# Part of the routing moved into sweep 3, two input pieces loaded later, and a shorter first piece in the last stage

## The chip, the cores and the metric

The kernel runs on one NeuronCore of a Trainium2 chip. The metric is the device time of one execution in microseconds (us), median of several runs. The engines are TensorE (PE, with its weight loads PEld), VectorE (DVE), ScalarE (ACT) and GpSimd (POOL); SyncE (SP) here only issues DMA transfers.

## What is computed

A graph layer, a top-2 mixture of eight experts, a second graph layer, and a small integer operation on the result. `_layernorm` is over the 256 columns of a row.

```python
x = x + gnn0(_layernorm(x), adj, W0, b0)          # A @ (x @ W + b) / deg[:, None]
x = x + ffn(_layernorm(x)[None], Wg, bg, W1, b1, W2, b2)[0]
x = x + gnn1(_layernorm(x), adj, WL, bL)          # relu(adj_norm @ x @ W.T + b)
x = x + shift_op(_layernorm(x)[None])[0]
# in ffn:
gate_scores = jax.nn.softmax(xt @ Wg + bg, axis=-1)
topk_scores, topk_idx = jax.lax.top_k(gate_scores, 2)
topk_scores = topk_scores / jnp.sum(topk_scores, axis=-1, keepdims=True)
h = gelu(xt @ W1[e] + b1[e]);  expert_out = h @ W2[e] + b2[e]
```

x is 4096 x 256, adj is 4096 x 4096, float32.

## The kernel before

Rows of x are held as 32 tiles of 128 rows. The program has three blocks, with a barrier of all engines between two of them.

The first block makes graph layer one in four sweeps. A sweep makes the sums of 1024 output rows (8 tiles): TensorE goes over the 32 tiles of adj (512 KB each, loaded by SP into a ring of 8) and multiplies them with the normalised rows `feat0`, held as a high and a low f16 half. Sweep 0 makes `feat0` on the way: x comes in five pieces (4, 4, 8, 8, 8 tiles); of each piece VectorE makes the statistics and normalised rows, ScalarE the high half, GpSimd the low half. SP's queue is written out by hand: `X_AFTER` says behind which adj tile a piece of x is issued, and `ROOT_BEFORE` before which row ScalarE makes a piece's square root. The sums of a sweep are split in two halves (ScalarE `sum_hi`, VectorE `sum_lo`) and projected with W0 during the next sweep; the projections of sweep 2 (tiles 16 to 23) run behind tiles 20 to 27 of sweep 3. Those of sweep 3 (tiles 24 to 31) come after it, when VectorE has made `sum_lo` from `sum_hi` (L579, `low_sums(3)`). While it waits TensorE runs 16 idle matmuls (`keep_busy`).

A projection has ten more columns than its 256; eight of them carry a part of the expert logits and go to `tail`. The other part of the logits, from x itself, is in `xg`. After a group of eight tiles `row_roots` makes the factor `r1` of its layer norm; in its middle it gives `ve` to ScalarE (L749) and gets the root back. VectorE's order at the end of sweep 3 is `row_roots(2)`, `degrees` of the last group (three small instructions, L714 to L716), `low_sums(3)`, eight tiles of `add_late_mean` (L733) and `row_stats`, `row_roots(3)`, and then the routing.

The routing begins with the logits of all 32 tiles, 256 columns to a partition (8 experts by 32 tiles), and two rounds of `pick` (L804 to L819), which find the best and the second best expert. `logit`, `key` and `score` lie in PSUM banks. ScalarE copies the eight columns of `tail` into `logit` first (L1005). TensorE then makes the ranks of the tokens, VectorE the place of each token, and sixteen batches of one-hot matrices, until `tokens` is ready; GpSimd waits for it and starts the first gathers of the next block (L535, L342).

Beside it ScalarE and GpSimd go on by their own orders. From the last `ve` on ScalarE runs two W2 units (`high_middle`), rows 16 to 23 (`normalise`, `high_late_row`), two units, rows 24 to 31, and the other units. GpSimd makes the low half of each: L514, two instructions of 1024 columns for two units, and L495, one of 256 columns for a row. Both read two operands in SBUF.

The second block runs the experts over slots of 256 tokens. The third makes graph layer two in five groups (8, 8, 8, 4, 4 tiles). It reloads x in the same five `PIECES`, and has the chain of statistics, root, `scaled` (VectorE), high half (ScalarE) and low half (GpSimd, L1554) again, where GpSimd also puts in the self edges of the first eight tiles (L1540, L1542). `scaled` has two buffers: VectorE scales tile n only when GpSimd has done tile n - 2. TensorE needs the low half of tile j to begin tile j.

Of the kernel before, what the change touches and what calls it, by code (L numbers as in the profile page):

```python
# [72 lines left out]
def program(nc, x, adjT, W0, b0, Wg, bg, W1, b1t, W2, b2, WL, bL, identity, upper, out):  # L73
# [176 lines left out]
    rows_early = w("rows_early", [P, 4, 2 * D], F16)  # L250
    xn8 = w("xn8", [P, G, D], F32)
    w = Region(SUM_AT, SUMS_END)
    row_hot = [w(f"row_hot{i}", [P, HOTS, P], F16) for i in range(2)]
    blk_hot = [w(f"blk_hot{i}", [P, HOTS, BLOCKS], F16) for i in range(2)]
    chosen16 = [w(f"chosen16{k}", [P, NT, E], F16) for k in range(2)]
    mix = w("mix", [P, NT, E], F32)
    running = w("running", [P, NT + 1, E], F32)
    best = [w(f"best{k}", [P, NT], F32) for k in range(2)]
    nearest = w("nearest", [P, NT], F32)
    end_at = w("end_at", [P, E], F32)  # L260
# [7 lines left out]

    logit, key, score = (pb[i][:, 0:NT * E].rearrange("p (n e) -> p n e", e=E) for i in (3, 4, 5))
    count_ps = pb[6][:, 0:P]  # L270
# [5 lines left out]
    small = iter(range(0, 512, NT))  # L276
    gap_top = pb[7][:, (at := next(small)):at + NT]
    share = [pb[7][:, (at := next(small)):at + NT] for k in range(3)]
# [48 lines left out]
    def over_tiles(ap):  # L327
        return ap.unsqueeze(1).broadcast_to([P, NT, E])
# [19 lines left out]
    PIECES = ((0, 4), (4, 4), (8, 8), (16, 8), (24, 8))  # L348
    X_AFTER = {0: 1, 3: 2, 8: 3, 14: 4}
    ROOT_BEFORE = {0: 0, 4: 1, 7: 2, 15: 3, 22: 4}  # L350

    with nc.Block(no_gpsimd_drain=True) as block:
# [188 lines left out]
        def _(v):  # L541
# [258 lines left out]
            st = Steps(v, sem("v_route"))  # L800
            v.wait_ge(sem("numbers_taken"), 4 + 2 * E)
            v.wait_ge(sem("xg_taken"), 2)
            v.wait_ge(sem("gates_copied"), 1)
            st.link(v.tensor_tensor(logit, logit, over_experts(rdeg[:, :]), ALU.mult))  # L804
            st.link(v.tensor_tensor(logit, logit, xg[:, :, :], ALU.add))
            st.link(v.tensor_tensor(logit, logit, over_experts(r1[:, :]), ALU.mult))
            st.link(v.tensor_tensor(logit, logit, over_tiles(bg_all[:, :]), ALU.add))

            def pick(scores, best, one_hot):
                st.link(v.tensor_reduce(best, scores, AX, ALU.max))  # L810
                st.link(v.tensor_tensor(key, scores, over_experts(best), ALU.is_equal))
                st.link(v.tensor_tensor(key, key, over_tiles(rev[:, :]), ALU.mult))
                st.link(v.tensor_reduce(nearest[:, :], key, AX, ALU.max))
                st.wait()
                v.tensor_tensor(one_hot, key, over_experts(nearest[:, :]), ALU.is_equal).then_inc(sem("choice_ready"), 1)

            pick(logit, best[0][:, :], chosen16[0][:, :, :])
            v.wait_ge(sem("choice_ready"), 1)
            st.link(v.scalar_tensor_tensor(out=score, in0=chosen16[0][:, :, :], scalar=-BIG, in1=logit, op0=ALU.mult, op1=ALU.add))  # L819
            pick(score, best[1][:, :], chosen16[1][:, :, :])  # L820
            st.link(v.tensor_reduce(gap_top, score, AX, ALU.max))
            st.wait()
            v.tensor_tensor(gap[:, :], gap_top, best[0][:, :], ALU.subtract).then_inc(sem("gap_ready"), 1)
# [4 lines left out]
            v.wait_ge(sem("choice_ready"), 2)  # L828
            st.wait()
# [75 lines left out]
        def _(a):  # L905
# [123 lines left out]
        def _(pe):  # L1029
# [106 lines left out]
            pe.wait_ge(sem("choice_ready"), 1)  # L1136
            pe.wait_ge(sem("x1_ready"), NT)
# [365 lines left out]
    with nc.Block(no_gpsimd_drain=True) as block:  # L1503

        @block.sync
        def _(sp):
            def load_x2(g):
                at, tiles = PIECES[g]
                sp.dma_start(x_sb[:, at:at + tiles, :], x2_v[:, at:at + tiles, :]).then_inc(sem(f"x_loaded{g}"), 16)
# [7 lines left out]
            load_x2(0)  # L1517
            for g in range(1, len(PIECES)):
# [46 lines left out]
        def _(v):  # L1565
# [88 lines left out]
            st = Steps(v, sem("v_norm2"))  # L1654
            for g, (at, tiles) in enumerate(PIECES):
                v.wait_ge(sem(f"x_loaded{g}"), 32)
# [26 lines left out]
        def _(a):  # L1683
# [17 lines left out]

            for g, (at, tiles) in enumerate(PIECES):
# [76 lines left out]
```

## Time and profile before

| | us |
|---|---|
| median of 3 runs | 1015.05 (1014.02 to 1015.86) |
| profiled execution, its own time | 1014.64 |
| its span, first to last instruction | 1012.8 |
| PE busy | 927.3 (92%) |
| DVE busy | 604.5 (60%) |
| POOL busy | 428.3 (42%) |
| ACT busy | 400.9 (40%) |
| mean granted TensorE clock | 0.961 of full |

The profile lists busy time, waits and their releasers for one execution. A timeline row gives the start, the time from first start to last end, engine, line, operation, and in brackets the idle time before it and what ended it. Times count from the first instruction. The granted clock is 1.00 at 2.4 GHz and 0.50 at 1.2 GHz. Sweep 3 ends at 264.5 us, the last gathers of the first block are issued at 322.44 us and the last stage begins at 734 us.

### The profile page before, as it was taken

To read this page: it belongs to the slowest core of one execution; us is meant where nothing else is said; L and a number is where in the kernel's file an instruction comes from. 1 tells how busy PE (TensorE), PEld (TensorE's weight loads), DVE (VectorE), ACT (ScalarE), POOL (GpSimd) and SP (SyncE) were. 2 spreads that over 40 slices of the span, in tenths; PEclk is the share of its full clock that TensorE was granted. 3 is DMA by queue.
4 is the path that set the end of the run, shared out by engine and by line. 5 is a ranking of instruction groups with operands and counts; after the bars stand their busy time and mean duration, and the time that the engine had idled before them with its cause. 6 is when DMAs were issued, how large, how long until landed. Compare 5 with 4: busy or idle time off the path is not lost. (4 is left out here: it accounts for less than half of the span.)

```text
span 1012.8 us, 21659 instructions
## 1 busy us (share of the span) xinstructions
PE 927.3 (92%) x6593; PEld 608.3 (60%) x6594; DVE 604.5 (60%) x1938; ACT 400.9 (40%) x837; POOL 428.3 (42%) x437
## 2 busy tenths in 40 slices
PE   8999999999715999999999999999279999999994
PEld 5354445444403898998898899898234454544442
DVE  7736996897797666566556556556167151341644
ACT  5858777477795532322332332333013101010111
POOL 3464756515585254455455455455454300200110
PEclk9999999999956999999999999999789999999997
DMA  9989999899876433233233332323299979875770
GB/s 334 411 302 344 345 357 332 282 360 367 281 243 185 120 50 53 43 49 53 45 47 53 47 47 53 47 42 53 43 361 402 358 236 327 264 262 167 242 264 25
DMA packets 91578, 199.93 MB, mean 197 GB/s; under 512 B 14241, under 2 KB 47266, under 8 KB 91394
## 3 DMA queue, kind: packets, MB, share of 16 engines
q1 hardware_dynamic: 74482, 168.37, 47.0%
q0 software_dynamic: 17040, 30.87, 15.0%
q8 instruction: 29, 0.48, 0.2%
q14 instruction: 27, 0.22, 0.1%
HBM read 177.05 MB, written 22.16 MB: 197 GB/s over the span
## 5 line engine op out<-in xcount | busy, mean ns | idle before, releaser
L1041 PE MATMUL bank<-adj_f,feat 128*128 128x512 f16 x1024 | 237.8, 387 | 4.1 <-DMA adj_f<-in_adjT 2.7
L1327 ACT ACTIVATE act_f<-bank,b_sb 128x256 f32<-128x256 f32 (+1 forms) x312 | 122.5, 450 | 255.1 <-PE bank L1258 255.1
L1258 PE MATMUL bank<-rT,experts 128*128 128x256 f16 (+1 forms) x1872 | 191.2, 263 | 2.5 <-DVE rT L1366 2.5
L1270 PE MATMUL bank<-experts,act_h 128*128 (+1 forms) x1680 | 189.1, 273 | 0.0
L1728 PE MATMUL bank<-adj_g,feat 128*128 128x512 f16 x768 | 179.7, 388 | 1.2 <-POOL feat L1554 1.2
L1258 PEld LDWEIGHTS bank<-rT,experts 128*128 (+1 forms) x1872 | 168.8, 99 | 19.8 <-DVE rT L1366 2.9
L1041 PEld LDWEIGHTS bank<-adj_f,feat 128*128 128x128 f16 x1024 | 96.9, 96 | 129.9 <-DMA adj_f<-in_adjT 4.7
L1270 PEld LDWEIGHTS bank<-experts,act_h 128*128 128x128 f16 x1680 | 163.0, 98 | 18.3
L923 ACT ACTIVATE spent<-adj_f 128x1024 f16<-128x1024 f32 x128 | 135.1, 1055 | 23.3 <-DMA adj_f<-in_adjT 17.5
L1185 POOL DMA_INDIRECT x_rows<-y,token x70 | 113.4, 1621 | 63.9 <-issue 54.6
L1728 PEld LDWEIGHTS bank<-adj_g,feat 128*128 128x128 f16 x768 | 74.4, 97 | 94.5 <-issue 2.1
L1354 DVE TENSOR_TENSOR act_h<-act_f,act_h 128x512 f16<-128x512 f32 x140 | 97.1, 693 | 4.8
L646 DVE CUSTOM_DVE_ANT_0 products<-agg,wg_turned 128x256 f32<-128x256 f32 x192 | 98.3, 575 | 0.0
L342 POOL DMA_INDIRECT rows<-ln_rows,token x68 | 69.5, 1022 | 40.1 <-DVE gates L1361 22.3
L1352 DVE CAST act_h<-act_f 128x512 f16<-128x512 f32 x140 | 59.9, 428 | 24.5 <-PE bank L1270 23.9
L1591 DVE SCALAR_TENSOR_TENSOR agg_lo<-bank,agg_hi 128x512 f16<-128x512 f32 x16 | 10.0, 683 | 94.0 <-ACT agg_hi L1690 94.0
L466 POOL TENSOR_SCALAR unit_f<-unit_f 128x1024 f32<-128x1024 f32 x16 | 45.9, 2866 | 42.3 <-ACT experts L928 42.3
L1728 PE MATMUL bank<-adj_early,feat 128*128 128x512 f16 x256 | 59.6, 388 | 0.9 <-issue 0.9
L1361 DVE COPY gates<-rows (+1 forms) x32 | 5.9, 184 | 83.7 <-PE bank L1241 83.7
L192 ACT ACTIVATE std<-mv,eps_col 128x8 f32<-128x8 f32 x10 | 3.0, 301 | 131.5 <-DVE mv L1573 131.5
L1198 POOL COPY token<-tokens 128x10 int32 (+1 forms) x35 | 11.8, 338 | 86.2 <-DMA x_rows<-y,token 86.2
L1540 POOL TENSOR_TENSOR adj_g<-adj_g,grow 128x128 f32<-128x128 f32 x24 | 11.2, 465 | 83.0 <-DMA adj_g<-in_adjT 83.0
(274 smaller groups left out, 986.5 us busy)
## 6 DMA issues: line engine op xcount, KB each, us to landing
adj_f<-in_adjT SPq DMA_DIRECT2D x128, 512.0 KB, 7.1
adj_g<-in_adjT SPq DMA_DIRECT2D x72, 512.0 KB, 6.0
adj_early<-in_adjT SPq DMA_DIRECT2D x24, 512.0 KB, 6.8
adj_g<-in_adjT SPq DMA_DIRECT2D x48, 256.0 KB, 3.1
unit_f<-in_W SPq DMA_DIRECT2D x16, 512.0 KB, 6.8
stage<-in_W SPq DMA_DIRECT2D x12, 512.0 KB, 6.0
x_ring<-in_x POOLq DMA_DIRECT2D x16, 256.0 KB, 6.9
x_rows<-agg SPq DMA_DIRECT2D x4, 1024.0 KB, 8.4
```

Source lines behind the costliest of these rows:

```text
L342: pool.indirect_dma_start(rows[:, r, :], None, ln_rows[:, :], bass.IndirectOffsetOnAxis(ap=indices[:, at + r:at + r + 1], axis=0)).then_in ...
L466: pool.tensor_scalar(unit_f[u % 2][:, :], unit_f[u % 2][:, :], WS, None, ALU.mult).then_inc(sem("unit_scaled"), 1)
L646: gate_steps.did(v.tensor_tensor_reduce(out=products[:, k % PRODUCTS, :], in0=agg[:, n, :], in1=wg_turned[:, e, :], scale=1.0, scalar=0.0, ...
L923: a.activation(spent[:, :], adj_f[j % RING][:, :], ACT.Copy, accum_out=degp[:, s, j:j + 1]).then_inc(sem("deg_ready"), 1)
L1041: last = pe.matmul(mine(s)[ib * DC + c][:, :], feat0[:, j, h, c * P:(c + 1) * P], adj_0[j % RING][:, ib * HALF_SWEEP:(ib + 1) * HALF_SWEEP ...
L1185: pool.indirect_dma_start(x_rows[:, :], bass.IndirectOffsetOnAxis(ap=token[:, r:r + 1], axis=0), y[:, r, :], None, compute_op=ALU.add).the ...
L1258: last = pe.matmul(pb[2 + q][:, k * SLOT + at:k * SLOT + at + width], w1_part(mine_e * DC + (f // FQ * W2_UNIT0 + c), wh)[:, (f % FQ) * P: ...
L1270: last = pe.matmul(pb[6 + r][:, 0:D], act_h[:, ah, f, r * P:(r + 1) * P], experts[:, ds(e[r] * DC + (W2_UNIT0 + f // UH), 1), wh, (f % UH) ...
L1327: last = a.activation(act_f[q][:, k, at:at + width], pb[2 + q][:, k * SLOT + at:k * SLOT + at + width], ACT.Gelu, bias=b1_sb[:, ds(mine_e ...
L1352: v.tensor_copy(hi, act_f[q][:, :, :]).then_inc(sem("act_hi_ready"), 1)
L1354: v.tensor_tensor(act_h[:, 1, 2 * q:2 * q + 2, :], act_f[q][:, :, :], hi, ALU.subtract).then_inc(sem("act_h_ready"), 1)
L1728: last = pe.matmul(mine(s)[ib * DC + c][:, :], feat[:, j, h, c * P:(c + 1) * P], adj_1[b][:, ib * HALF_SWEEP:(ib + 1) * HALF_SWEEP], start ...
```

## The change

Three edits. First, the logits and both picks of tiles 0 to 23 are made by VectorE in sweep 3, between `row_roots(2)` and `degrees`, and those of tiles 24 to 31 after `row_roots(3)`; this is one function `choose`, which works in SBUF on `tail`, `xg`, `scores` and, for `nearest`, `dinv`. The reduction L821 and ScalarE's copy L1005 are gone; TensorE waits for the third and fourth choice. Second, in sweep 0 the x pieces 3 and 4 are issued behind adj tiles 10 and 16, where it was 8 and 14. Third, the last stage loads x in pieces of 2, 6, 8, 8 and 8 tiles.

```diff
-    X_AFTER = {0: 1, 3: 2, 8: 3, 14: 4}
+    X2_PIECES = ((0, 2), (2, 6), (8, 8), (16, 8), (24, 8))
+    X_AFTER = {0: 1, 3: 2, 10: 3, 16: 4}
...
+            def choose(first, end, turn):
+                tiles, n = slice(first, end), end - first
+                logit, held, second = xg[:, tiles, :], tail[:, tiles, 2:2 + E], scores[:, 0:n, :]
...
+                def pick(values, k):
+                    choice.link(v.tensor_reduce(best[k][:, tiles], values, AX, ALU.max))
+                    choice.link(v.tensor_tensor(held, values, by_tile(best[k]), ALU.is_equal))
+                    choice.link(v.tensor_tensor(held, held, by_expert(rev[:, :]), ALU.mult))
+                    choice.link(v.tensor_reduce(nearest[:, tiles], held, AX, ALU.max))
+                    v.tensor_tensor(chosen16[k][:, tiles, :], held, by_tile(nearest), ALU.is_equal).then_inc(sem("choice_ready"), 1)
+
+                choice.link(v.tensor_tensor(held, held, by_tile(rdeg), ALU.mult))
+                choice.link(v.tensor_tensor(logit, held, logit, ALU.add))
+                choice.link(v.tensor_tensor(logit, logit, by_tile(r1), ALU.mult))
+                choice.link(v.tensor_tensor(logit, logit, by_expert(bg_all[:, :]), ALU.add))
+                pick(logit, 0)
+                v.wait_ge(sem("choice_ready"), 2 * turn + 1)
+                choice.link(v.scalar_tensor_tensor(out=second, in0=chosen16[0][:, tiles, :], scalar=-BIG, in1=logit,
+                                                   op0=ALU.mult, op1=ALU.add))
+                pick(second, 1)
...
             row_roots(2)
...
+            choose(0, 3 * G, 0)
             degrees(3 * G, G)
             low_sums(3)
...
-            st.link(v.tensor_tensor(logit, logit, over_experts(rdeg[:, :]), ALU.mult))
...
+            choose(3 * G, NT, 1)
+            v.tensor_tensor(gap[:, :], best[1][:, :], best[0][:, :], ALU.subtract).then_inc(sem("gap_ready"), 1)
...
-            a.wait_ge(sem("tail_taken"), G)
-            a.copy(logit, tail[:, :, 2:2 + E]).then_inc(sem("gates_copied"), 1)
```

VectorE at the end of sweep 3, before. The first row is the end of `row_roots(2)` and the last is `low_sums(3)`; `gates` holds the shift of the rows here.

```order
L757 TENSOR_TENSOR r_73<-nt_81,rstd 128x8
L759 SCALAR_TENSOR_TENSOR gates<-mv,r_73 128x8
L714 TENSOR_REDUCE dg<-degp 128x8
L715 TENSOR_SCALAR dg<-dg 128x8
L716 RECIPROCAL rdeg<-dg 128x8
L579 SCALAR_TENSOR_TENSOR sum_lo<-bank,sum_hi 128x512 x4
```

The same place after the change:

```order
L767 SCALAR_TENSOR_TENSOR gates<-mv,r_73 128x8
L817 TENSOR_TENSOR tail<-tail,rdeg 128x24x8
L818 TENSOR_TENSOR xg<-tail,xg 128x192
L819 TENSOR_TENSOR xg<-xg,r_73 128x192
L820 TENSOR_TENSOR xg<-xg,bg_all 128x192
L811 TENSOR_REDUCE best_157<-xg 128x24
L812 TENSOR_TENSOR tail<-xg,best_157 128x24x8
...
L815 TENSOR_TENSOR chosen_161<-tail,dinv 128x192
L722 TENSOR_REDUCE dg<-degp 128x8
L723 TENSOR_SCALAR dg<-dg 128x8
L724 RECIPROCAL rdeg<-dg 128x8
L587 SCALAR_TENSOR_TENSOR sum_lo<-bank,sum_hi 128x512 x4
```

Fifteen instructions of 192 columns (24 tiles by 8 experts) now stand between `row_roots(2)` and `degrees`, and so ahead of `low_sums(3)`.

VectorE at the start of the routing, before (`bank` is PSUM):

```order
L804 TENSOR_TENSOR bank<-bank,rdeg 128x256
L805 TENSOR_TENSOR bank<-bank,xg 128x256
L806 TENSOR_TENSOR bank<-bank,r_73 128x256
L807 TENSOR_TENSOR bank<-bank,bg_all 128x256
L810 TENSOR_REDUCE best_165<-bank 128x32
...
L815 TENSOR_TENSOR chosen_162<-bank,nearest 128x256
L821 TENSOR_REDUCE bank<-bank 128x32
L823 TENSOR_TENSOR gap<-bank,best_165 128x32
```

The same place after the change:

```order
L817 TENSOR_TENSOR tail<-tail,rdeg 128x8x8
L818 TENSOR_TENSOR xg<-tail,xg 128x64
L819 TENSOR_TENSOR xg<-xg,r_73 128x64
L820 TENSOR_TENSOR xg<-xg,bg_all 128x64
L811 TENSOR_REDUCE best_157<-xg 128x8
...
L815 TENSOR_TENSOR chosen_161<-tail,dinv 128x64
L847 TENSOR_TENSOR gap<-best_158,best_157 128x32
```

Fifteen linked instructions remain here, now of 64 columns, and no operand is in PSUM.

SP's queue in sweep 0, before (`agg<-in_x` is a piece of x, `adj_f` a tile of adj; the first row is tile 7):

```order
L369 DMA adj_f_124<-in_adjT 128x1024
L369 DMA adj_f_117<-in_adjT 128x1024
L362 DMA agg<-in_x 128x8x256
L369 DMA adj_f_118<-in_adjT 128x1024
L369 DMA adj_f_119<-in_adjT 128x1024
L369 DMA adj_f_120<-in_adjT 128x1024
L369 DMA adj_f_121<-in_adjT 128x1024
L358 DMA unit_f_137<-in_W 128x1024
L369 DMA adj_f_122<-in_adjT 128x1024
L369 DMA adj_f_123<-in_adjT 128x1024
L362 DMA agg<-in_x 128x8x256
L369 DMA adj_f_124<-in_adjT 128x1024
```

And after the change, from tile 8 on:

```order
L377 DMA adj_f_117<-in_adjT 128x1024
L377 DMA adj_f_118<-in_adjT 128x1024
L377 DMA adj_f_119<-in_adjT 128x1024
L370 DMA agg<-in_x 128x8x256
L377 DMA adj_f_120<-in_adjT 128x1024
L377 DMA adj_f_121<-in_adjT 128x1024
L366 DMA unit_f_137<-in_W 128x1024
L377 DMA adj_f_122<-in_adjT 128x1024
L377 DMA adj_f_123<-in_adjT 128x1024
L377 DMA adj_f_124<-in_adjT 128x1024
L377 DMA adj_f_117<-in_adjT 128x1024
L370 DMA agg<-in_x 128x8x256
```

The pieces stand two adj tiles later; the total ahead of tile 11 and of tile 17 is the same.

## Rows read from the trace of the kernel before

**Rows 1.** VectorE, timeline at the end of sweep 3: start us, us, instruction.
```profile
261.07 0.62 DVE L759 SCALAR_TENSOR_TENSOR gates<-mv,r 128x8 f32<-128x8 f32 x1
262.00 0.21 DVE L714 TENSOR_REDUCE dg<-degp 128x8 f32<-128x32 f32 x1 [0.31 <-ACT spent L923]
...
265.42 2.48 DVE L579 SCALAR_TENSOR_TENSOR sum_lo<-bank,sum_hi 128x512 f16<-128x512 f32 x4 [2.52 <-ACT sum_hi L936]
...
272.77 0.47 DVE L733 SCALAR_TENSOR_TENSOR agg<-bank,rdeg,x_ring 128x256 f32<-128x256 f32 x1
```

**Rows 2.** The timeline of TensorE's matmuls, the last eight projections.
```profile
266.77 0.29 PE L198 MATMUL bank<-w0s,sum_hi 128*128 128x266 f16 x1 [0.28 <-DVE sum_lo L579]
...
272.11 0.28 PE L198 MATMUL bank<-w0s,sum_hi 128*128 128x266 f16 x1
```

**Rows 3.** The timeline of VectorE, two linked instructions of 192 columns.
```profile
215.74 0.36 DVE L666 TENSOR_TENSOR products<-mv,wg_total 128x192 f32<-128x192 f32 x1
216.13 0.36 DVE L668 TENSOR_TENSOR xg<-xg,products 128x192 f32<-128x192 f32 x1
```

**Rows 4.** The timeline of VectorE, first and last instruction of the top-2 choice.
```profile
276.36 0.43 DVE L804 TENSOR_TENSOR bank<-bank,rdeg 128x256 f32<-128x256 f32 x1
...
282.99 0.42 DVE L815 TENSOR_TENSOR chosen<-bank,nearest 128x256 f16<-128x256 f32 x1
```

**Rows 5.** The timeline of GpSimd during and after the routing.
```profile
277.14 4.21 POOL L514 TENSOR_TENSOR experts<-stage,experts 128x1024 f16<-128x1024 f32 x2 [4.17 <-ACT stage L998]
281.31 3.18 POOL L495 TENSOR_TENSOR rows_late<-xn,rows_late 128x256 f16<-128x256 f32 x5
...
313.77 4.21 POOL L514 TENSOR_TENSOR experts<-stage,experts 128x1024 f16<-128x1024 f32 x2 [3.27 <-ACT stage L998]
...
320.45 0.19 POOL L535 COPY first_tokens<-tokens 128x8 int32<-128x8 int32 x1 [1.25 <-DVEq L894]
```

**Rows 6.** The timelines of GpSimd and VectorE, where the two meet, twice.
```profile
115.62 2.18 POOL L468 TENSOR_TENSOR experts<-unit_f,experts 128x1024 f16<-128x1024 f32 x1
115.74 2.34 DVE L646 CUSTOM_DVE_ANT_0 products<-agg,wg_turned 128x256 f32<-128x256 f32 x1
...
231.99 1.31 POOL L495 TENSOR_TENSOR rows_early<-xn,rows_early 128x256 f16<-128x256 f32 x2
231.64 1.94 DVE L725 SCALAR_TENSOR_TENSOR agg<-agg,rdeg,x_ring 128x256 f32<-128x256 f32 x1
```

**Rows 7.** TensorE in the last stage: timeline; windows (us, busy, granted clock, DMA, GB/s).
```profile
996.96 0.28 PE L198 MATMUL bank<-wLs,agg_hi 128*128 128x256 f16 x1 [2.01 <-DVE agg_lo L1591]
...
997.50:998.00 0.50, 0.50 (x6) 0.81 0.00 0
...
1001.00:1001.50 0.50, 0.42 (x3) 0.78 0.00 0
```

**Rows 8.** Sweep 0: the page's GB/s by slices; TensorE's timeline.
```profile
GB/s 334 411 302 344 345 357 332 282 360 367 281 243 185 120 50 53 43 49 53 45 47 53 47 47 53 47 42 53 43 361 402 358 236 327 264 262 167 242 264 25
...
28.63 3.79 PE L1041 MATMUL bank<-adj_f,feat 128*128 128x512 f16 x16 [1.44 <-DMA adj_f<-in_adjT]
...
40.16 12.82 PE L1041 MATMUL bank<-adj_f,feat 128*128 128x512 f16 x56 [0.15 <-DMA adj_f<-in_adjT]
```

**Rows 9.** Start of the last stage: the timelines of VectorE, GpSimd and TensorE.
```profile
738.01 0.42 DVE L1660 BATCH_NORM_STATS2 stats<-x_sb 128x6 f32<-128x256 f32 x1 [13.86 <-issue]
...
741.27 0.73 DVE L1666 TENSOR_SCALAR scaled<-x_sb,mv,scale 128x256 f32<-128x256 f32 x2
...
748.62 0.73 DVE L1666 TENSOR_SCALAR scaled<-x_sb,mv,scale 128x256 f32<-128x256 f32 x2
...
742.20 0.67 POOL L1554 TENSOR_TENSOR feat<-scaled,feat 128x256 f16<-128x256 f32 x1 [7.04 <-ACT feat L1706]
...
743.78 0.67 POOL L1554 TENSOR_TENSOR feat<-scaled,feat 128x256 f16<-128x256 f32 x1
...
758.90 14.67 PE L1728 MATMUL bank<-adj_g,feat 128*128 128x512 f16 x64 [1.17 <-POOL feat L1554]
```

More of the change, by code:

```diff
@@ L100, in program @@
     ident16 = keep("ident16", [P, P], F16)
+    SCORES_AT = keep.at
     before = keep("before", [P, P], F32)
@@ L104, in program @@
     ones16 = keep("ones16", [P, P], F16)
+    BEST_AT = keep.at
     zeros16 = keep("zeros16", [P, P], F16)
@@ L139, in program @@
     table = keep("table", [P, 64], I32)
+    CHOSEN_AT = keep.at
     grow = keep("grow", [P, P], F32)
@@ L145, in program @@
     square = keep("square", [P, NT], F32)
+    CHOSEN_END = keep.at
     step16_i = keep("step16_i", [P, 16], I32)
@@ L251, in program @@
     xn8 = w("xn8", [P, G, D], F32)
+    w = Region(BEST_AT, BEST_AT + P * 2)
+    best = [w(f"best{k}", [P, NT], F32) for k in range(2)]
+    w = Region(SCORES_AT, SCORES_AT + 2 * P * 4)
+    scores = w("scores", [P, 3 * G, E], F32)
+    w = Region(CHOSEN_AT, CHOSEN_END)
+    chosen16 = [w(f"chosen16{k}", [P, NT, E], F16) for k in range(2)]
+    nearest = dinv
     w = Region(SUM_AT, SUMS_END)
@@ L254, in program @@
     blk_hot = [w(f"blk_hot{i}", [P, HOTS, BLOCKS], F16) for i in range(2)]
-    chosen16 = [w(f"chosen16{k}", [P, NT, E], F16) for k in range(2)]
     mix = w("mix", [P, NT, E], F32)
     running = w("running", [P, NT + 1, E], F32)
-    best = [w(f"best{k}", [P, NT], F32) for k in range(2)]
-    nearest = w("nearest", [P, NT], F32)
     end_at = w("end_at", [P, E], F32)
@@ L267, in program @@
     row = w("row", [P, 2, NT], F32)
-    logit, key, score = (pb[i][:, 0:NT * E].rearrange("p (n e) -> p n e", e=E) for i in (3, 4, 5))
+    key, score = (pb[i][:, 0:NT * E].rearrange("p (n e) -> p n e", e=E) for i in (4, 5))
     count_ps = pb[6][:, 0:P]
@@ L276, in program @@
     small = iter(range(0, 512, NT))
-    gap_top = pb[7][:, (at := next(small)):at + NT]
     share = [pb[7][:, (at := next(small)):at + NT] for k in range(3)]
@@ L789, in _, with by_tile, by_expert @@
                     row_stats(2 * G + k - 1)
-            row_roots(2)
+            choice = Steps(v, sem("v_choice"))
+            def choose(first, end, turn):
+                tiles, n = slice(first, end), end - first
+                logit, held, second = xg[:, tiles, :], tail[:, tiles, 2:2 + E], scores[:, 0:n, :]
+                def by_tile(ap):
+                    return ap[:, tiles].unsqueeze(2).broadcast_to([P, n, E])
+                def by_expert(ap):
+                    return ap.unsqueeze(1).broadcast_to([P, n, E])
+                def pick(values, k):
[13 more added lines that the diff above has]
+                pick(second, 1)
+                v.wait_ge(sem("choice_ready"), 2 * turn + 2)
+            row_roots(2)
+            v.wait_ge(sem("numbers_taken"), 4 + 2 * E)
+            v.wait_ge(sem("xg_taken"), 2)
+            v.wait_ge(sem("agg_taken"), 2 * OT + 4)
+            v.wait_ge(sem("shift_ready"), 2)
+            choose(0, 3 * G, 0)
             degrees(3 * G, G)
@@ L800, in _ @@
             st = Steps(v, sem("v_route"))
-            v.wait_ge(sem("numbers_taken"), 4 + 2 * E)
-            v.wait_ge(sem("xg_taken"), 2)
-            v.wait_ge(sem("gates_copied"), 1)
-            st.link(v.tensor_tensor(logit, logit, over_experts(rdeg[:, :]), ALU.mult))
[L805 to L823, printed above, removed]
+            v.wait_ge(sem("tail_taken"), G)
+            v.wait_ge(sem("shift_ready"), 3)
+            choose(3 * G, NT, 1)
+            v.tensor_tensor(gap[:, :], best[1][:, :], best[0][:, :], ALU.subtract).then_inc(sem("gap_ready"), 1)
             st.did(v.memset(one[:, :], 1.0))
@@ L1507, in load_x2 @@
             def load_x2(g):
-                at, tiles = PIECES[g]
+                at, tiles = X2_PIECES[g]
                 sp.dma_start(x_sb[:, at:at + tiles, :], x2_v[:, at:at + tiles, :]).then_inc(sem(f"x_loaded{g}"), 16)
@@ L1517, in _ @@
             load_x2(0)
-            for g in range(1, len(PIECES)):
+            for g in range(1, len(X2_PIECES)):
                 load_x2(g)
@@ L1654, in _ @@
             st = Steps(v, sem("v_norm2"))
-            for g, (at, tiles) in enumerate(PIECES):
+            for g, (at, tiles) in enumerate(X2_PIECES):
                 v.wait_ge(sem(f"x_loaded{g}"), 32)
@@ L1700, in make_rows @@
                                  ).then_inc(sem("out_made"), 1)
-            for g, (at, tiles) in enumerate(PIECES):
+            for g, (at, tiles) in enumerate(X2_PIECES):
                 norm_root(a, "n2_", g)
```

5 lines of the change are left out of this document (2 added, 3 removed).

## The prediction, made before the changed kernel ran

> **What bounds the kernel now.** The page comes first: TensorE is busy for 92% of the span, so a time is gained or lost only where TensorE waits. The waits of TensorE then give the places, and the timelines of the single engines, read side by side, give the reasons. The change touches three of them.
>
> In sweep 0 TensorE stands 1.44 us before tile 9 and 0.15 us before tile 15, each time for an adj tile whose transfer stands behind a piece of x [rows 8]. At the end of sweep 3 it has hardly a wait: VectorE ends `row_roots(2)` at 261.7, is idle for 0.31 us before `degrees` and 2.52 us before `low_sums(3)`, which ScalarE releases at 265.42 [rows 1], and TensorE stands 0.28 us before the first of the last eight projections [rows 2]. From there to the end of the block VectorE sets the pace, since its last add starts at 272.77 [rows 1] and the last projection matmul at 272.11 [rows 2]. In the routing TensorE has almost nothing to do, and the path is VectorE's own chain: the choice takes from 276.36 to 283.41 (282.99 and 0.42), 15 linked steps of 0.47 us [rows 4]. It ends at `tokens`, for which GpSimd has waited 1.25 us when it copies them at 320.45 [rows 5]. So GpSimd's own chain, which comes from ScalarE's, has 1.25 us of slack, no more. In the last stage TensorE runs without a gap from tile 8 on, at 758.90, after a wait of 1.17 us for GpSimd's low half [rows 9].
>
> **The choice of tiles 0 to 23, moved into sweep 3.** It is 15 linked instructions of 192 columns. Two linked instructions of this size start 0.39 us apart [rows 3], so the choice takes 5.85 us. It can start when L759 is done, at 261.69, and ends at 267.5. `degrees` is three instructions like the one of 0.21 us, some 0.7 us with their waits [rows 1]. Then `low_sums(3)` starts at 268.2 and not at 265.42. The gap that the move fills is 3.7 us long, what is put there takes 6.5 us. **Term 1: +2.8 us.** Low bound +2.4, if L759 isn't held to 0.62 us (its neighbours take 0.17 to 0.2); zero is excluded, since 5.85 us don't fit. Queued behind it on VectorE are `sum_lo`, the last eight adds, `row_roots(3)` and with it ScalarE's root, so ScalarE's and GpSimd's chains move by the same 2.8 us.
>
> TensorE now stands about 3.1 us before these eight projections (0.28 and 2.8). What that does to its clock is seen in the last stage: after a wait of 2.01 us the granted clock fell within a microsecond of the restart (0.81 over 997.5 to 998) and came back at about 1001.2 [rows 7], some 3.3 us at 1.2 GHz. There 3.3 us do the work of 1.65. Here TensorE is about 0.4 us ahead of VectorE at the end (which starts the last add 0.66 us after the start of the last matmul of 0.28 us). **Term 2: 1.65 less 0.4, +1.2 us.** Low bound 0, if the clock holds; I take the fall, because the idle time is longer than in the row.
>
> **The choice of tiles 24 to 31, after row_roots(3).** By width alone it gets cheaper: 0.43 us at 256 columns and 0.36 at 192 [rows 3, 4] give about 0.22 at 64, 0.26 with the wait, so 15 steps are 3.9 us where 7.05 stood, a gain of 3.1. But eleven of the fifteen now read two operands in SBUF, where before one was in PSUM. GpSimd is working then: 0.78 us after the routing's first instruction it starts two instructions of 1024 columns (4.21 us), and five of 256 columns (3.18 us) follow without a gap [rows 5]. They hang on ScalarE's root, thus move with VectorE and meet the choice at the same place. What such a meeting costs is seen twice: an instruction of VectorE with two SBUF operands, else 0.41 us long, took 2.34 us when it started 0.12 us after GpSimd's of 2.18 us, and ended when that had ended; another took 1.94 us and outlasted two of GpSimd's in a row, 1.31 us together [rows 6]. The L759 of 8 columns and 0.62 us is the same [rows 1].
>
> If VectorE gets in once between two of GpSimd's: three steps are free (0.78 us), then eight instructions with two SBUF operands each wait for one of GpSimd's, two of 2.1 us and six of 0.64, and take 0.22 themselves; the reductions lie beside. 0.8 + 4.2 + 3.8 + 1.8 = 10.6 us against 7.05. **Term 3: +3.5 us.** Low bound -3.1 (no meeting). High bound: if VectorE waits through a run without gaps, it stands until 8.1 us after the start (277.14 and 281.31 with 3.18, counted from 276.36), with eleven steps left, which end at 12 us or, behind the next two long ones, at 16.5: +5 to +9.4. I take the first, since the instruction that met the long one did get in directly behind it.
>
> The Trainium skill says in "SBUF — State Buffer", section "Who interferes with whom", that a VectorE instruction with two SBUF inputs contends with a GpSimd one that reads SBUF, and that the one issued first holds the pair of ports for its whole instruction. That agrees with the 2.34 us; the 1.94 us is longer than this rule alone gives. By the rule the sum is that with +3.5, by the second row it is that with +9.4.
>
> The rest of the routing works in PSUM with one operand and keeps its length. The removed L821 and L1005 lie beside other work. SP's mix store comes no earlier than its place behind the unit loads.
>
> **The x pieces.** Every transfer ahead of tile 9 loses a piece of 1 MB, so its wait goes. But tiles 11 and 17 have the same bytes ahead as before. At 411 GB/s [rows 8] 512 KB take 1.28 us; tile 15 came at 40.1, so tile 17 comes at 42.7, where TensorE (1.83 us a tile, 12.82 for seven) would have begun it at 43.8. **Term 4: -0.9 us**, at most 1.1 by this, at most 1.6 by the two waits, and at least -0.4, as ScalarE must now wait about 1 us for the statistics of the later piece before it makes row 15. The rest of the sweeps is TensorE's own pace and moves along.
>
> **The first piece of two tiles.** Its statistics are two instructions and two aggregates shorter (0.84 of the 3.26 us from 738.01 to 741.27 [rows 9]), and half a load comes perhaps 0.8 us sooner. VectorE then goes on with six tiles (about 4.3 us, by the 3.26 for four and 0.4 for each more, and some meeting with GpSimd) and GpSimd idles. Tile 8 waits for `scaled` 7, thus for the low half of tile 5. Before, that was 738.0 + 3.26 + 1.6 (to 742.87) + 1.58 for tile 1, 748.62 + 1.6 + 1.58 = 751.8. Now it is 737.2 + 2.42 + 0.8 + 4.3 + 1.6 + 3 x 1.58 = 751.1. **Term 5: -0.7 us**, from -1.4 to +0.2 (the load no sooner).
>
> **The sum.** 2.8 + 1.2 + 3.5 - 0.9 - 0.7 = +5.9 us on the profiled execution's 1014.64 (span 1012.8 and 1.84 around it), 1020.5. The median is 0.4 above that execution, so I say 1020.9.
>
> **The rivals.** *GpSimd doesn't hold VectorE* (the small instructions slip in). Then VectorE ends the routing 0.3 us sooner, and GpSimd's chain, 2.8 us later, less its 1.25 us of slack, sets the end: +1.55 - 1.6 = 0, 1015.0, with the fallen clock 1016.2. For it: 64 columns are short. Against it: L759 has 8 columns and was held. Chance 0.18. *VectorE waits through whole runs:* 5.9 + 1.5 to 5.9, 1022.4 to 1026.8. Chance 0.17. *Faster:* only if the choice fits the gap of sweep 3, which needs steps of 0.2 us instead of 0.39; from below 2.8 us for all fifteen the choice after it, unhindered, gives 3.1 us, of which the slack lets 1.25 through, and with terms 4 and 5 that makes -2.9, 1012.2. Nothing in the rows speaks for it: 0.04. *The forecast*, with or without the clock's fall: 0.61, its own range 1018 to 1022.5.
>
> About 0.2%, 2 us, is what a measurement of this kernel can tell from no change. The range reaches from the first rival to the top of the second: 1015.6 to 1026.5. Slower 0.78, same 0.18, faster 0.04.
>
> **What would show it.** `sum_lo` of sweep 3 starts 2.8 us later against the end of TensorE's sweep; TensorE's wait before the last eight projections is 3 us and the clock falls in them; the choice of 64 columns takes 9 to 12 us and holds instructions of 0.6 and of 2 us; GpSimd's wait before L535 is longer than 1.25 us. The wait before tile 9 is gone and one of about 0.5 us stands before tile 11 or 17; tile 8 of the last stage starts 0.7 us sooner after the block's begin. Wrong would be a choice of 4 us, or a `low_sums(3)` that still waits for ScalarE.

## The result and the profile after

The changed kernel takes 1020.19 us, the median of 6 executions (1017.95 to 1022.03), against 1014.53 for the kernel before, now also of 6 (1012.33 to 1015.86). The two medians stand 5.7 us apart. The comparison of executions, by which every ratio below is meant, gives 1.0048, 95% interval 1.0034 to 1.0062, which is 4.9 us. The forecast was +5.9 and 1020.9. Two executions of several milliseconds (3928.86 us of choice16, 5469.23 us of the kernel before) are left out of ratios and medians. The profiled execution took 1018.16 us (span 1016.1 against 1012.8): 3.3 us more in this pair. The rows below are from it.

TensorE's timeline in sweep 0, where [rows 8] had waits of 1.44 us before tile 9 and 0.15 us before tile 15, and at the sweep's end:

```profile
23.23 7.40 PE L1062 MATMUL bank<-adj_f,feat 128*128 128x512 f16 x32 [1.03 <-DMA adj_f<-in_adjT]
...
42.41 9.21 PE L1062 MATMUL bank<-adj_f,feat 128*128 128x512 f16 x40 [0.27 <-DMA adj_f<-in_adjT]
...
263.15 1.97 PE L209 MATMUL bank<-w0s 128*128 128x266 f16 x16
268.35 0.29 PE L202 MATMUL bank<-w0s,sum_hi 128*128 128x266 f16 x1 [3.22 <-DVE sum_lo L587]
...
273.69 0.28 PE L202 MATMUL bank<-w0s,sum_hi 128*128 128x266 f16 x1
```

The first of these rows is tile 7 and the second tile 17: the waits before tiles 9 and 15 are gone, and 0.27 us stand before tile 17. The keep-busy matmuls (L209) start where the sums of sweep 3 end: at 263.15 against 264.52 before. TensorE then stands 3.22 us, against 0.28 in [rows 2]. VectorE's timeline says why (the answer to [rows 1]):

```profile
259.70 0.62 DVE L767 SCALAR_TENSOR_TENSOR gates<-mv,r 128x8 f32<-128x8 f32 x1
260.46 0.36 DVE L817 TENSOR_TENSOR tail<-tail,rdeg 128x192 f32<-128x192 f32 x1
...
265.93 0.36 DVE L815 TENSOR_TENSOR chosen<-tail,dinv 128x192 f16<-128x192 f32 x1
266.32 0.21 DVE L722 TENSOR_REDUCE dg<-degp 128x8 f32<-128x32 f32 x1
...
267.01 2.48 DVE L587 SCALAR_TENSOR_TENSOR sum_lo<-bank,sum_hi 128x512 f16<-128x512 f32 x4
```

The early choice takes 5.86 us to the start of `degrees`, and from L767 to `sum_lo` no row of VectorE shows an idle time any more. `sum_lo` starts 3.86 us behind the last sum, before 0.90. The clock was granted in full in these projections in this execution (windows: time, busy PE, PEld, DVE, ACT and POOL, granted clock, DMA share, GB/s):

```profile
268.00:272.00 4.00, 3.65 (x33) 3.11 (x34) 3.96 (x13) 1.78 (x6) 3.60 (x2) 1.00 1.09 384
```

The late choice, in VectorE's timeline, with GpSimd's two instructions beside it (the answers to [rows 4] and [rows 5]):

```profile
278.10 0.23 DVE L817 TENSOR_TENSOR tail<-tail,rdeg 128x64 f32<-128x64 f32 x1
...
278.88 2.05 DVE L820 TENSOR_TENSOR xg<-xg,bg_all 128x64 f32<-128x64 f32 x1
280.96 0.22 DVE L811 TENSOR_REDUCE best<-xg 128x8 f32<-128x64 f32 x1
281.22 1.79 DVE L812 TENSOR_TENSOR tail<-xg,best 128x64 f32<-128x64 f32 x1
283.04 0.59 DVE L813 TENSOR_TENSOR tail<-tail,rev 128x64 f32<-128x64 f32 x1
...
286.44 0.54 DVE L815 TENSOR_TENSOR chosen<-tail,dinv 128x64 f16<-128x64 f32 x1
...
290.07 2.10 DVE L862 TENSOR_TENSOR own_lead<-own_at,base 128x8 f32<-128x8 f32 x1
...
278.72 4.21 POOL L522 TENSOR_TENSOR experts<-stage,experts 128x1024 f16<-128x1024 f32 x2 [7.11 <-ACT stage L1021]
282.88 3.19 POOL L503 TENSOR_TENSOR rows_late<-xn,rows_late 128x256 f16<-128x256 f32 x5
...
290.02 4.21 POOL L522 TENSOR_TENSOR experts<-stage,experts 128x1024 f16<-128x1024 f32 x2 [1.23 <-ACT stage L1021]
...
325.40 0.19 POOL L543 COPY first_tokens<-tokens 128x8 int32<-128x8 int32 x1 [4.60 <-DVEq L917]
```

An instruction of 64 columns that meets nothing takes 0.23 us. L820 starts 0.16 us after the first long one of GpSimd and ends when that one has ended; L812 is held by the second. The choice takes 8.88 us, not the 3.9 of its width. Later L862, of 8 columns and with two SBUF operands as before the change, starts 0.05 us behind the next long one and takes 2.10 us. Before, it started during a short instruction of GpSimd, ended with it, and took 0.41 us (VectorE's and GpSimd's timelines of the kernel before):

```profile
286.82 0.41 DVE L839 TENSOR_TENSOR own_lead<-own_at,base 128x8 f32<-128x8 f32 x1
...
286.54 0.67 POOL L495 TENSOR_TENSOR rows_late<-xn,rows_late 128x256 f16<-128x256 f32 x1 [0.27 <-ACT rows_late L955]
```

GpSimd now waits 4.60 us for the tokens, against 1.25.

In the last stage VectorE's statistics, TensorE's tile 8 and the last projections (the answers to [rows 9] and [rows 7]):

```profile
742.49 0.42 DVE L1681 BATCH_NORM_STATS2 stats<-x_sb 128x6 f32<-128x256 f32 x1 [12.71 <-issue]
744.94 0.74 DVE L1687 TENSOR_SCALAR scaled<-x_sb,mv,scale 128x256 f32<-128x256 f32 x2
...
763.17 12.17 PE L1749 MATMUL bank<-adj_g,feat 128*128 128x512 f16 x53 [0.71 <-POOL feat L1575]
...
1001.23 0.28 PE L202 MATMUL bank<-wLs,agg_hi 128*128 128x256 f16 x1 [2.01 <-DVE agg_lo L1612]
...
1002.00:1004.00 2.00, 2.00 (x19) 1.57 (x16) 1.63 (x4) 0.00 (x0) 0.00 (x0) 1.00 0.00 0
```

Counted from the issue of the stage's first x (739.72, before 734.06), the statistics begin at 2.77 us (before 3.95) and tile 8 at 23.45 (24.84). After the same wait of 2.01 us as in [rows 7] the clock did not fall here.

The two profiled executions, cut at five points, with those of the experiments (us; the last sum is the start of L209, "tokens" GpSimd's copy of them, the issue that of the last stage's first x; "P" is from the first to the last start of the eight projections, 5.34 at full clock):

| kernel | last sum | to sum_lo | P | sum_lo to tokens | tokens to issue | issue to end | span |
|---|---|---|---|---|---|---|---|
| before | 264.52 | 0.90 | 5.34 | 55.03 | 413.61 | 278.74 | 1012.8 |
| after | 263.15 | 3.86 | 5.34 | 58.39 | 414.32 | 276.38 | 1016.1 |
| after_again | 263.06 | 3.85 | 6.62 | 59.67 | 413.76 | 276.46 | 1016.8 |
| x_only | 263.48 | 0.91 | 5.35 | 55.04 | 414.04 | 279.13 | 1012.6 |
| x2_only | 264.50 | 0.90 | 5.34 | 55.04 | 413.85 | 276.21 | 1010.5 |
| both_pieces | 263.13 | 0.91 | 5.35 | 55.03 | 413.96 | 276.37 | 1009.4 |
| choose_only | 264.19 | 3.85 | 5.34 | 58.41 | 414.26 | 278.99 | 1019.7 |
| choose_busy | 266.95 | 3.86 | 5.34 | 58.41 | 412.71 | 279.07 | 1021.0 |
| ballast | 264.64 | 3.65 | 5.34 | 55.18 | 414.16 | 279.27 | 1016.9 |
| busy44 | 265.80 | 4.09 | 5.34 | 58.41 | 414.55 | 276.45 | 1019.3 |
| own_psum | 263.74 | 3.89 | 7.01 | 58.04 | 414.25 | 276.28 | 1016.2 |
| choice_own_psum | 263.78 | 3.86 | 7.01 | 56.23 | 415.43 | 276.40 | 1015.7 |
| choice16 | 263.39 | 0.90 | 5.35 | 54.63 | 413.24 | 276.44 | 1008.6 |
| mix_held | 263.08 | 0.91 | 5.35 | 54.61 | 412.70 | 277.70 | 1009.0 |

Before against after: -1.37 + 2.96 + 3.36 + 0.71 - 2.36 = +3.3 us. The time from the tokens to the issue is 412.70 to 415.43 us over the fourteen profiles, so a difference of 0.7 there can be chance.

### The profile page after: what moved, and what is told of

It is laid out like the page before. It is cut to its first block and busy times, and to the rows that moved or that the text cites. A ratio compares the mean times of both kernels' runs of the same rounds, so it can differ in the third digit from the quotient of the medians.

```text
span 1016.1 us, 21672 instructions
## 1 busy us (share of the span) xinstructions
PE 929.3 (91%) x6593; PEld 608.9 (60%) x6594; DVE 609.7 (60%) x1952; ACT 401.2 (39%) x836; POOL 432.0 (43%) x437
## 5 line engine op out<-in xcount | busy, mean ns | idle before, releaser
L654 DVE CUSTOM_DVE_ANT_0 products<-agg,wg_turned 128x256 f32<-128x256 f32 x192 | 95.1, 557 | 0.0
```

The costliest lines, as they stand in the source:

```text
L654: gate_steps.did(v.tensor_tensor_reduce(out=products[:, k % PRODUCTS, :], in0=agg[:, n, :], in1=wg_turned[:, e, :], scale=1.0, scalar=0.0, ...
```

## The experiments

My theory was the list of terms; the rivals are beside each. Ratios are to the kernel before, with their 95% intervals.

**The parts alone.** x_only is the kernel before with the first line, x2_only with the two-tile piece, both_pieces with both; choose_only is the changed kernel without either:

```
-    X_AFTER = {0: 1, 3: 2, 8: 3, 14: 4}
+    X_AFTER = {0: 1, 3: 2, 10: 3, 16: 4}
...
+    X2_PIECES = ((0, 2), (2, 6), (8, 8), (16, 8), (24, 8))
```

> The kernel before with one edit: the x pieces 3 and 4 are issued behind tiles 10 and 16 (X_AFTER of the changed kernel). Theory A (the two traces): TensorE ends the sums of sweep 3 1.4 us earlier, as it did in the changed kernel (263.15 against 264.52), and all behind it comes forward by that: 1.4 us less than before, ratio about 0.9986. Theory B (my Term 4): 0.9 us less. Rival C: the gain is given back at the next thing that is set by the flow of data, and the time is within 0.3 us of before; then the keep-busy matmuls at the end of sweep 3 start no earlier than 264.3 or the start of expert block 2 does not move from 324.4.

Measured: 1013.85 us, ratio 0.9985 (0.9976 to 0.9995), 1.5 us less. The sums end at 263.48, 1.04 us earlier. By the ratio the gain reaches the end; in the pair of profiles the spans differ by 0.2 us only, since the two later stretches were 0.4 us longer each in this one. Theories A and B both lie in the interval, C does not.

> The kernel before with one edit: the last stage's x begins with a piece of two tiles, then six. Theory A (the two traces): the first statistics come 1.2 us earlier behind the load's issue and TensorE's tile 8 1.4 us earlier, and the whole stage is as much shorter: 1.4 us less than before, ratio about 0.9986. Theory B (my Term 5): 0.7 us less. Rival C: the last stage is bound elsewhere (its flags stream in at the same rate) and the time is within 0.3 us of before. Where the clock falls in the last projections, this kernel's profile can stand up to 1 us from these numbers; the comparison of many executions decides.

Measured: 1012.92 us, ratio 0.9983 (0.9974 to 0.9992), 1.7 us less: Theory A lies in the interval, B just outside it (0.9993). The profile shows 2.5 us less in the stage. 1.5 of it lies ahead of the last projections. The rest is the clock in them: they take 1.6 us less, of which 0.6 is given back behind them. The windows of this kernel, then those of before (the same columns as above):

```profile
996.00:998.00 2.00, 2.00 (x21) 1.79 (x19) 1.30 (x3) 0.00 (x0) 0.00 (x0) 1.00 0.00 0
```

```profile
998.00:1000.00 2.00, 2.00 (x11) 1.40 (x10) 1.13 (x3) 0.00 (x0) 0.00 (x0) 0.50 0.00 0
```

21 matmuls in 2 us at 1.00, 11 at 0.50. Over all profiles the clock fell there in five of five kernels with the old piece (from the first to the last start 3.96 to 4.19 us) and in one of nine with the new one (mix_held, 4.18; the others 2.52 to 2.53). Why the clock goes with the piece, no run shows.

> The changed kernel with the old x pieces in both stages, so that the choice of the top two in two turns is alone. Theory A (terms as the traces of before and after show them: 2.96 at the end of sweep 3, 3.2 from the start of the routing to the token table, about 0.6 at the barrier, nothing for the clock): 6 to 7 us more than before, ratio 1.006 to 1.007, with the early choice ending in a TensorE wait of about 3.2 us and the choice of 64 columns at about 8.9 us. Theory B (my Terms 1 to 3 as forecast): 7.5 us more. Rival C: the pieces were worth nothing and the choice costs only what the changed kernel lost in all, 5 to 5.7 us.

Measured: 1024.56 us, ratio 1.0098 (1.0083 to 1.0114), 9.9 us more; its profiled execution, 1021.74 us, shows 6.9. The times from the last sum to `sum_lo` and on to the tokens are those of the changed kernel to 0.1 us, as Theory A has it; the median lies above all three forecasts. The profiled execution was the fastest of the four.

> The kernel before with both edits of the x pieces and the choice as it was. Theory A: the two gains as measured apart (ratios 0.9985 and 0.9983) add: 3.2 us less than before, ratio 0.9968; the choice then costs 8.1 us in the changed kernel, near the 10 us of the choice alone. Theory B (my Terms 4 and 5): 1.6 us less, 0.9984. Rival C: the gain of one is lost when the other is there, ratio 0.9983 or more.

Measured: 1012.09 us, ratio 0.9975 (0.9965 to 0.9985), 2.5 us less. All three theories (0.9968, 0.9984, 0.9983 or more) touch the interval, so it doesn't tell them apart. The profile shows 1.4 us in sweep 0 and 2.4 in the last stage.

**The early choice as a mere load** (15 times, linked, behind `row_roots(2)` of the kernel before; `spill` isn't read):

```
+                st.link(v.tensor_tensor(spill[:, :, :], xg[:, 0:3 * G, :], tail[:, 0:3 * G, 2:2 + E], ALU.mult))
```

> The kernel before with 15 linked VectorE instructions more, at the place of the early choice: each multiplies 192 columns of xg with the tails and writes memory that nobody reads; the routing is as before. It puts a price on the place alone. Theory A: 15 instructions at 0.39 us and nothing saved behind them, 2.9 us more than before (ratio 1.0029), low parts of the sums begin 3.9 us behind TensorE's last sum against 0.90, the clock stays at 1.00 through the eight projections. Theory B (my Terms 1 and 2): 4.0 us more, the clock is below 1.00 in the projections. Rival C: the 2.9 us are taken up by GpSimd's and ScalarE's work of the routing, which then ends last, and the time is under 1 us more.

Measured: 1020.59 us, ratio 1.0062 (1.0049 to 1.0076). In the profile `sum_lo` starts 2.75 us later than before, TensorE waits 3.02 us, and the tokens come 3.02 us later: Theory A holds at the place, and so does its clock of 1.00; rival C fell. The span is 4.1 us longer, the median 5.5 and the ratio says 6.3: more than the place shows, and more than Theories A (2.9) and B (4.0) allow.

**Is the excess the clock?** First the changed kernel with its wait filled, then it once more, then the choice alone with the wait filled:

```
-            keep_busy(pe, late[0], 16)
+            keep_busy(pe, late[0], 44)
```

> The changed kernel with 44 keep-busy matmuls in place of 16 ahead of the last eight projections: the 28 more, at 0.11 us each (16 took 1.97 us), fill the 3.22 us in which TensorE waits there, and write a bank that is written again. Asked: six runs of the changed kernel spread over 1017.95 to 1022.03 us and the profiled one, whose clock stayed at 1.00 in that stage, is one of its two fastest. Theory A (my Term 2 in another form: in the slower executions the clock falls in or behind that wait): the runs come together near 1018, the median is 1.5 to 2 us less than that of the changed kernel, ratio to before 1.003 to 1.0035. Theory B (the clock is lost elsewhere, or not at all): median and spread as those of the changed kernel, 1020.2 and ratio 1.005; the profiled execution shows the projections at the same pace.

Measured: 1019.94 us, ratio 1.0052 (1.0040 to 1.0065): Theory B. The wait is 0.30 us, the pace unchanged, the median too. Its profile is no clean pair with the changed kernel's: TensorE waited 3.25 us before tile 7 of sweep 0, and the sums ended 2.65 us later.

> The changed kernel once more, beside the others on one chip, for a second profile and more executions: its profiled execution of 1018.16 us stands 2 us below its median. Theory A (my Term 2 in part: the clock falls in the last eight projections in some executions, as in the kernel with both PSUM edits, where they took 7.0 us against 5.3): a median of 1019 to 1020.5 and, if this execution is one of those, windows below 1.00 between 4 and 9 us behind the last sum and 1.7 us more there. Theory B (memory is slower in the first 40 us in some executions, where TensorE waited 3.25 us for flags in one profile and 0.66 in another): the spread comes from sweep 0, and a slower execution shows its last sum later than 263.2 us.

Measured: 1019.88 us, ratio 1.0049 (1.0036 to 1.0062). This time the clock fell, in TensorE's timeline and windows:

```profile
268.25 0.40 PE L202 MATMUL bank<-w0s,sum_hi 128*128 128x266 f16 x1 [3.22 <-DVE sum_lo L587]
...
267.00:269.00 2.00, 0.75 (x4) 0.54 (x5) 2.00 (x4) 2.00 (x3) 1.71 (x1) 0.62 1.04 355
269.00:271.00 2.00, 2.00 (x11) 1.35 (x10) 0.88 (x2) 0.26 (x2) 2.00 (x2) 0.53 1.09 388
271.00:273.00 2.00, 2.00 (x20) 1.70 (x18) 1.90 (x8) 0.34 (x2) 0.49 (x1) 1.00 1.09 386
```

The projections took 6.62 us instead of 5.34, and all of the 1.28 us arrives at the tokens. This agrees with Theory A. B's sign, a later last sum, is absent here (263.06), though busy44 and choose_busy show it. The same program and the same wait: once the clock holds, once it falls. Of the six profiles with a wait of 3.0 to 3.3 us here three show the fall (6.62, 7.01, 7.01), of the eight without it none.

> The kernel with the choice alone (old x pieces in both stages) and 44 keep-busy matmuls in place of 16 ahead of the last eight projections, so that TensorE does not stand still for 3.2 us. By now three of six profiles with that wait showed the granted clock at 0.50 for some 3 us behind it (projections of 6.6 to 7.0 us against 5.3) and none of the seven without it. Theory A (the clock's fall in part of the executions is what lifts the choice alone from +6.9 us in its profile to a ratio of 1.0098): projections of 5.3 us in the profile, no execution above 1023.5 us, ratio 1.007 to 1.0085. Theory B (its other executions were long for a reason elsewhere): ratio 1.009 or more again, projections at full clock all the same.

Measured: 1022.67 us, ratio 1.0071 (1.0058 to 1.0084), no execution above 1023.04. That is Theory A's range, below the 1.0098 of the choice alone, though the two intervals still touch. But filling the wait did nothing for the changed kernel, so the clock's fall is shown as a cost that some executions have, and not as what lifts the median.

**What holds VectorE.** own_psum copies `own_at` to PSUM while VectorE waits for the ranks; choice_own_psum does so and puts the scores and marks of the late choice into banks 3 to 5:

```
+            st.did(v.tensor_copy(own_ps, own_at[:, :]))
...
-            st.link(v.tensor_tensor(own_lead[:, :], own_at[:, :], base[:, :], ALU.subtract))
+            st.link(v.tensor_tensor(own_lead[:, :], own_ps, base[:, :], ALU.subtract))
...
+                    logit, held, second = (pb[i][:, 0:n * E].rearrange("p (n e) -> p n e", e=E) for i in (3, 4, 5))
```

> The changed kernel with one edit: own_at is copied to PSUM while VectorE waits for the ranks, so that own_lead (8 columns), which took 2.10 us behind GpSimd's split, reads one operand from SBUF and one from PSUM. Theory A: own_lead takes 0.17 us, as in the kernel with both PSUM edits, the late choice keeps its 8.9 us, and from the last sum to the copy of the tokens it takes 1.9 us less than the changed kernel's 62.25. The ratio to before is about 1.003, and inside what the comparison can tell from 1.0048. Rival B: the time is given back further on, the copy of the tokens stays within 0.5 us of 62.25 us behind the last sum.

Measured: 1018.20 us, ratio 1.0037 (1.0018 to 1.0057), which can't be told from 1.0048; Theory A had said so. `own_lead` took 0.17 us, the choice 8.9 as before. From the last sum to the tokens it took 61.93 us with the projections 1.67 us longer; without that 60.3, 2.0 less than after.

> The changed kernel with two edits: the choice of tiles 24 to 31 keeps its scores and marks in PSUM (its first instruction alone still reads two operands in SBUF), and own_at is copied to PSUM while VectorE waits for the ranks, so that own_lead (8 columns) reads one operand of each kind. Theory A (two SBUF operands meet GpSimd's shared access, one does not): the 15 instructions take 0.22 to 0.35 us each, the choice about 4.3 us against 8.9, own_lead 0.2 us against 2.10: 6.5 us less work on VectorE, of which at most 4.6 us come forward, for GpSimd's split of the last units then ends last: 4 to 4.6 us less than the changed kernel, 1 us above before to equal with it (ratio 0.9995 to 1.001). Rival B: half of that or less (ratio 1.0025 or more); then what held VectorE was not the access that it shares with GpSimd.

Measured: 1017.30 us, ratio 1.0032 (1.0019 to 1.0045). In VectorE's timeline the same instructions as above, now with at most one SBUF operand from the second on, and then `gap`, which keeps two:

```profile
280.31 0.23 DVE L822 TENSOR_TENSOR bank<-tail,rdeg 128x64 f32<-128x64 f32 x1
...
281.11 0.23 DVE L825 TENSOR_TENSOR bank<-bank,bg_all 128x64 f32<-128x64 f32 x1
...
281.63 0.23 DVE L817 TENSOR_TENSOR bank<-bank,best 128x64 f32<-128x64 f32 x1
...
283.99 0.22 DVE L820 TENSOR_TENSOR chosen<-bank,dinv 128x64 f16<-128x64 f32 x1
284.25 0.93 DVE L852 TENSOR_TENSOR gap<-best,best 128x32 f32<-128x32 f32 x1
...
288.00 0.17 DVE L868 TENSOR_TENSOR own_lead<-bank,base 128x8 f32<-128x8 f32 x1
```

2.05 and 1.79 us became 0.23, the choice 3.9 us instead of 8.88, while GpSimd's two long instructions ran from 280.93 to 285.14, and `gap` was held until the second ended (0.93 us, against 0.19 before). So the two SBUF operands were what met GpSimd, as Theory A has it. Its time failed all the same: it said 0.9995 to 1.001, and the ratio is in Rival B's range. Of the 5 us that VectorE saves over own_psum, 1.8 arrive at the tokens, for GpSimd's wait there was only 2.70 us and its own chain got 0.87 us longer (below).

**A better place.** choice16 is choice_own_psum with an early choice of 16 tiles that stands behind `row_roots(1)`:

```
             row_roots(1)
...
+            choose(0, 2 * G, 0)
...
-            choose(3 * G, NT, 1)
+            choose(2 * G, NT, 1)
```

> The same two edits, and the early choice is of tiles 0 to 15 and stands behind the roots of tiles 8 to 15 (at about 241 us), where VectorE waits 1.2 to 1.65 us for TensorE before each of the next tiles; the late one is of 16 tiles, 128 columns, in PSUM. Theory A: the 5 us of the early choice fit into those waits, the low parts of the sums begin 0.9 us behind TensorE's last sum again, the late choice takes 5 us, and GpSimd's chain ends last: 1.3 us less than before from it, 3.2 us less from the pieces (by the runs of each alone), 4 to 4.5 us less than before in all (ratio 0.9955 to 0.996). Rival B: VectorE holds the banks of tiles 16 to 19 too long, TensorE waits inside sweep 3, and 1 to 3 us of it are lost. Rival C: the pieces alone remain, 3.2 us less (0.9968).

Measured: 1011.77 us, ratio 0.9977 (0.9967 to 0.9988), level with the pieces alone. Theory A (0.9955 to 0.996) failed, and so did B; the result is Rival C in kind. The early choice cost nothing (`sum_lo` 0.90 us behind the last sum), the late one took 4.9 us. GpSimd's chain sets the end, and it got longer. ScalarE's timeline, of both_pieces and then of this kernel:

```profile
310.31 1.06 ACT L998 ACTIVATE experts<-stage 128x1024 f16<-128x1024 f32 x1 [3.59 <-DMA stage<-in_W]
```

```profile
311.43 1.06 ACT L1026 ACTIVATE experts<-stage 128x1024 f16<-128x1024 f32 x1 [4.46 <-DMA stage<-in_W]
```

A weight unit lands 0.87 us later, so of GpSimd's slack of 1.25 us 0.4 are left to gain. My suspect was the store of the mix weights, which now comes right behind the load. mix_held is choice16 with one wait more before that store:

```
             sp.wait_ge(sem("mix_ready"), 1)
+            sp.wait_ge(sem("middle_hi"), 2 * (LATE_UNIT0 - W2_UNIT0) - 3)
```

> The kernel with the early choice of tiles 0 to 15, with one wait more: SyncE holds the store of the mix weights until ScalarE has begun on the last pair of weight units. There the mix was ready 2 us earlier than in the kernel with both pieces alone, its store was issued at 304.67 us right behind the loads of the last two units, and ScalarE waited 4.46 us for these against 3.59. Theory A (the store's many small packets hold the loads up): ScalarE's wait is 3.6 us again, GpSimd's last split starts 0.9 us earlier, the copy of the tokens stands 54.6 to 54.8 us behind the last sum against 55.53, and the time is 0.9 us less, ratio to before about 0.997. Rival B: the loads were late for another reason, the wait stays at 4.4 us. Rival C: the store itself now ends last and GpSimd waits for it before the gather: no gain or a loss up to 2 us.

Measured: 1012.33 us, ratio 0.9974 (0.9964 to 0.9984). The store was issued at 312.21, behind the load's landing, and ScalarE still waited 4.42 us: Rival B, my theory fell. The late landing (4.42 to 4.46 us of waiting against 3.57 to 3.60) shows in the three kernels whose late choice is in PSUM and in no other; why stays open.

## Why the prediction was right, and where not

The side and the range held, and the two terms of the choice are the largest, as said. That the sum of +5.9 lies so near is luck in part. In the pair of profiles the total is +3.3: Term 2 is absent (1.2) and Term 5 brought 1.7 more than forecast. The executions then stand above that pair for reasons that are mostly open. By its steps:

**Term 1 (+2.8): right.** The traces show 2.96 (3.86 less 0.90), the load alone 2.75, and TensorE waits 3.22 us where 3.1 was said.

**Term 2 (+1.2): the mechanism is right in three of the six profiles with such a wait, as a cost of every execution it was not.** "I take the fall, because the idle time is longer than in the row" was the step that failed: longer idle time did not decide it. The profiled execution has no fall, after_again 1.28 us (1.2 was the forecast for a fall), own_psum and choice_own_psum 1.67.

**Term 3 (+3.5): the sum is right by two errors.** In the choice I let eight instructions wait, six of them for a whole short instruction; two were held long, as said, and six lost 0.1 to 0.4 us each. The scan (the first long step behind the choice) began 9.59 us after the choice's start where it had been 8.08: +1.5, not +3.5. That VectorE gets in between two back-to-back instructions of GpSimd is shown by L820, which ended at 280.93 while the second of the two ran on to 282.93, and by L812 behind that one. The other 1.7 us came from L862, against the sentence "The rest of the routing works in PSUM with one operand and keeps its length". That sentence was wrong: `own_at` and `base` are both in SBUF, and the shift moved L862 from a short GpSimd instruction onto a long one. The rival "GpSimd doesn't hold VectorE" fell, and so did that of whole runs. In the latter a step of the working is loose too: from 8.1 us, eleven steps of 0.26 end at 11, not at 12.

**Term 4 (-0.9): the mechanism right, the size 0.5 too small, within its bounds.** -1.37 between the two profiles, -1.5 (-0.5 to -2.4) by the ratio of x_only. The wait before tile 9 is 1.33 to 1.45 us in four of the five profiles with the old order (in the fifth a wait of 3.67 us stands before tile 7) and absent in all nine with the new one, where 0.24 to 0.54 us stand before tile 17. Part of any such difference is chance: the wait before tile 7, which the change doesn't touch, was 0.55 to 3.67 us over the fourteen profiles.

**Term 5 (-0.7): too small, -2.4 in the profile.** Tile 8 came 1.39 us sooner; the load's gain, put at 0.8, was 1.18. The 1.0 us more is the clock in the last projections, of which the prediction said nothing though [rows 7] showed its fall.

The sum of the terms as the profile has them is 2.96 + 0 + 3.2 - 1.37 - 2.36, and 0.7 to 0.9 from the tokens to the last stage. The comparison of executions gives 4.9, some 1.5 us more than the pair of profiles (the medians 2.4 more). The clock's fall behind the wait (1.3 to 1.7 us in half of the profiles) can be half of that; the rest is open, as is the excess of ballast and choose_only over their profiles. The profiled executions of ballast, choose_only and after_again were the fastest of their kernels, and that of the changed kernel the second fastest of six, so a profile alone understates these kernels' medians.

Nothing here beats both_pieces clearly: the pieces alone give 2.5 us, and the choice in two turns, put into real gaps and kept from GpSimd's way, gives nothing more.

## What to carry to other kernels

Work that is moved into a gap has to fit the gap as it is, not the engine's mean idle time: into a gap of 3.7 us went 6.7 us (260.32 to 267.01), and the rest stood before TensorE. Where a chain of small steps runs beside GpSimd, look at where each operand lies; one operand in PSUM made a step of 2.05 us one of 0.23. And list every later instruction with two SBUF operands too, since a shift of the chain moves it onto GpSimd's instructions.

## What was unexpected of the hardware

- The granted clock after the same wait of 3.22 us fell in one execution of one program (0.53 over 269 to 271) and held at 1.00 in another. After 2.01 us it fell in six of fourteen profiles, five of them those with the old piece in the last stage.
- An instruction of 8 columns took 2.10 us, and 0.17 us in own_psum. One SBUF operand is no full protection either: in choice_own_psum `tokens<-spare`, a TENSOR_SCALAR of 8 columns from SBUF to SBUF, took 1.44 us against 0.16 in the changed kernel. It ended at 322.67, as GpSimd's split did at 322.64 (318.43 and 4.21); in choice16 and mix_held it took 1.00 and 0.97 us and ended with the split too. The Trainium skill says in "SBUF — State Buffer", section "Who interferes with whom", that `tensor_scalar`, `copy` and `cast` can, with fitting operands, enter modes that take the pair of ports shared with GpSimd. That agrees:

```profile
321.23 1.44 DVE L921 TENSOR_SCALAR tokens<-spare 128x8 int32<-128x8 f32 x1
...
318.43 4.21 POOL L523 TENSOR_TENSOR experts<-stage,experts 128x1024 f16<-128x1024 f32 x2 [4.15 <-ACT stage L1027]
```
